# A planned transformer-and-experts kernel: two steps of the attention on GpSimd for four images, and a planner with stretched lengths and a table of bonuses

## What is computed

```python
x = x + linear_attention(ln_c(x))     # q softmax over 32 dims, k softmax over tokens, rmsnorm before and after
t = tokens(x)
t = t + moe(ln_t(t))                  # gate over 8 experts, the best two, 128 -> 256 -> gelu -> 128
out = images(t)
```

## Time and profile before

| | us |
|---|---|
| median of 3 runs | 775.15 (773.04 to 775.7) |
| profiled execution | 775.42 |
| its span | 773.7 |
| DVE busy in the span | 590.4 (76%) |
| PE busy | 654.0 (85%) |
| ACT busy | 536.7 (69%) |
| POOL busy | 481.6 (62%), of it 479.1 in 480 indirect DMAs |

### The profile page before, as it was taken

How to read it: one execution, slowest core, us unless ns; L and a number is a source line. 1 busy time by engine, 2 the same in 40 slices (tenths; PEclk the granted TensorE clock), 3 DMA queues, 4 the chain that set the end, 5 groups by cost and what they waited for, 6 DMA issues and landing times. The chain is left out here.

```text
span 773.7 us, 15758 instructions
## 1 busy us (share of the span) xinstructions
PE 654.0 (85%) x4074; PEld 545.7 (71%) x4074; DVE 590.4 (76%) x2178; ACT 536.7 (69%) x1388; POOL 481.6 (62%) x504
## 2 busy tenths in 40 slices
PE   4856489988989589999768899989689998699997
PEld 3534277866868367888566797876578887598896
DVE  5898989998999979997989899879885335642343
ACT  2633359667987549798737798868777775667775
POOL 1006553557646676776476777776777775677773
PEclk9978699998999889999978999999889999899999
DMA  6521466676756568697267788885499999537923
GB/s 170 154 90 62 148 204 199 204 235 175 224 155 198 171 208 238 198 316 216 100 202 214 223 284 244 272 269 166 124 276 323 319 325 322 185 102 216 315 81 109
DMA packets 110208, 159.28 MB, mean 206 GB/s; under 512 B 19216, under 2 KB 74536, under 8 KB 110120
## 3 DMA queue, kind: packets, MB, share of 16 engines
q1 hardware_dynamic: 93704, 126.58, 53.0%
q0 software_dynamic: 15360, 31.49, 13.5%
q10 hardware_dynamic: 1056, 0.22, 0.2%
HBM read 103.81 MB, written 57.02 MB: 208 GB/s over the span
## 5 line engine op out<-in xcount | busy, mean ns | idle before, releaser
L782 POOL DMA_INDIRECT rows_in<-xf_tok,row_of x240 | 243.4, 1014 | 199.0 <-DVE row_of L1343 108.3
L797 POOL DMA_INDIRECT y_rows<-rows_out,row_back x240 | 235.7, 982 | 81.1 <-issue 77.9
L1582 PE MATMUL y_ps<-wb,hid 128*128 128x128 f32 x1552 | 203.9, 278 | 13.7 <-ACT hid L899 12.5
L1582 PEld LDWEIGHTS y_ps<-wb,hid 128*128 128x128 f32 x1552 | 189.7, 192 | 27.9 <-ACT hid L899 22.7
L899 ACT ACTIVATE hid<-h_ps,wb 128x256 f32<-128x256 f32 x388 | 161.6, 474 | 52.8 <-PE h_ps L1572 32.1
L1572 PE MATMUL h_ps<-xt,wb 128*128 128x256 f32 x648 | 173.9, 396 | 6.4 <-DMA wb<-experts 4.5
L1572 PEld LDWEIGHTS h_ps<-xt,wb 128*128 128x128 f32 x648 | 116.6, 198 | 24.2 <-issue 6.0
L1410 DVE TENSOR_TENSOR yb<-y_ps,wb 128x256 f32<-128x256 f32 x162 | 68.1, 421 | 72.5 <-PE y_ps L1582 68.8
L1492 PE MATMUL ab<-wqkv_t,x_sb 128*128 128x392 f32 x256 | 105.6, 547 | 6.2 <-ACT qkv L837 5.7
L885 ACT ACTIVATE y_rows<-y_rows,share 128x128 f32<-128x128 f32 x240 | 83.2, 408 | 28.7 <-DMA y_rows<-rows_out,row_back 28.4
L837 ACT ACTIVATE qkv<-ab,root 128x392 f32<-128x392 f32 x128 | 71.2, 592 | 24.8 <-PE ab L1492 16.6
(11 more groups left out here) (195 smaller groups left out, 980.8 us busy)
## 6 DMA issues: line engine op xcount, KB each, us to landing
wb<-experts SPq DMA_DIRECT2D x162, 321.0 KB
xb<-rows_in SPq DMA_DIRECT2D x162, 128.0 KB
rows_out<-yb SPq DMA_DIRECT2D x162, 128.0 KB
rows_in<-zeros SPq DMA_DIRECT2D x69, 128.0 KB, 1.8
x_sb<-in_x_dram SPq DMA_DIRECT2D x16, 512.0 KB, 4.2
out_dram<-out_sb SPq DMA_DIRECT2D x32, 256.0 KB, 3.6
rows_in<-xf_tok,row_of POOLq DMA_INDIRECT x240
y_rows<-rows_out,row_back POOLq DMA_INDIRECT x240
```

What stands on the lines that cost most here:

```text
L782: pool.indirect_dma_start(out=rows_in[p % IN_BUFS], out_offset=bass.IndirectOffsetOnAxis(ap=row_of[:, n % X1_RING, k, t:t + 1], axis=0), i ...
L797: pool.indirect_dma_start(out=y_rows[:, r, k, :], out_offset=None, in_=rows_out[p % OUT_BUFS][0:BLOCKS[p] * ROWS, :], in_offset=bass.Indir ...
L1582: last = pe.matmul(y_ps[:, b % Y_BUFS, i * P:(i + 1) * P], hid[:, b % 2, k, i * P:(i + 1) * P], wb[:, r, HIDDEN + k * CH:HIDDEN + (k + 1) ...
```

## The change

1. For images 0 to 3 (`HELPED = 4`) `q_shift` and `q_norm` are issued on GpSimd instead of DVE: eight instructions in all. The planner takes them as 2.4 long there.
2. Every length is multiplied by a factor of its engine before planning (`PACE`).
3. `favour` adds a bonus per part of the program (`FAVOURED`, by image, group or dense expert) and one per kind of step (`FAVOURED_KIND`). The numbers go from -727 to 392.
4. A few steps get one more predecessor in the planner (`chain(...)`), the same step of the image before.

No other instruction is added or taken away. What each step computes and its buffers are unchanged.

```diff
+HELPED = 4
+PACE = {"PE": 1.08, "ACT": 1.1, "DVE": 1.1, "POOL": 1.035, "SP": 1.0}
+FAVOURED = {
+    "middle": (6.0, -68.8, 54.4, 21.4, 24.6, -37.8, 0.0, 0.9, -1.2, -12.9, 0.4, -89.8, -2.5, -1.3, 8.0, -19.7),
...
+FAVOURED_KIND = {
+    "C": 182.9, "D0": -2.6, "F1": 86.9, "F2": -26.0, "KB": -7.6, "KT": 3.4, "M": 4.9, "Q1": -38.6,
...
-        step("ACT", a("x_tok0"), 0.48, [a("X0")] + old("x1_1", TOK_RING), 0.2, table="any")
+        step("ACT", a("x_tok0"), 0.48, [a("X0")] + chain("x_tok1") + old("x1_1", TOK_RING), 0.2, table="any")
...
-        step("DVE", a("q_shift"), 1.14, [a("q_max")], 0.1)
+        step("POOL" if n < HELPED else "DVE", a("q_shift"), 2.4 if n < HELPED else 1.14, [a("q_max")], 0.12)
...
-        step("DVE", a("q_norm"), 1.14, [a("q_sum")], 0.1)
+        step("POOL" if n < HELPED else "DVE", a("q_norm"), 2.4 if n < HELPED else 1.14, [a("q_sum")], 0.12)
...
-        steps[name] = engine, length, more, [last_part.get(a, a) for a in after], bank, [last_part.get(a, a) for a in done or ()], table
+        steps[name] = engine, length * PACE[engine], more, [last_part.get(a, a) for a in after], bank, [last_part.get(a, a) for a in done or ()], table
...
 def favour(name):
 
-    if name[0] == "take":
-        return 500.0
-    return 0.0
+    part, i = part_of(name)
+    return (500.0 if name[0] == "take" else 0.0) + FAVOURED[part][i] + FAVOURED_KIND.get(name[0], 0.0)
...
+                if what == "q_shift":
+                    pool.wait_ge(s_q_max, n + 1)
+                    pool.tensor_tensor(queries(n), queries(n), stat_of_queries(0), ALU.subtract).then_inc(s_q_sub, 1)
+                if what == "q_norm":
+                    pool.wait_ge(s_q_sum, n * 2 + 2)
+                    pool.tensor_tensor(queries(n), queries(n), stat_of_queries(2), ALU.mult).then_inc(s_q_norm, 1)
```

More of the change, by code:

```diff
@@ L51 @@
 ROOT, SIZE, AHEAD = 10, 11, 0.15
+HELPED = 4
+PACE = {"PE": 1.08, "ACT": 1.1, "DVE": 1.1, "POOL": 1.035, "SP": 1.0}
+SETUP = ("load_w", "small", "experts", "ident", "center", "turn_w", "copy_w", "turn_s", "fold_gate", "fold_w", "turn_g", "fold_out",
+         "b1", "spare")
+EARLY = ("x_tok0", "x_tok1", "X0", "X1", "bn1_0", "bn1_1", "stats1", "load_x", "pair")
+LATE = ("logits0", "logits", "scores", "first", "exp", "choose", "count", "place", "xf0", "xf1", "stats2", "bn2_0", "bn2_1", "pair_r")
@@ new lines @@
+FAVOURED = {
+    "middle": (6.0, -68.8, 54.4, 21.4, 24.6, -37.8, 0.0, 0.9, -1.2, -12.9, 0.4, -89.8, -2.5, -1.3, 8.0, -19.7),
+    "back": (-15.2, -2.3, -62.5, -20.5, -51.5, 25.1, -86.2, -60.1, -8.0, 21.9, -17.7, -16.8, 4.1, 3.5, 93.8, 0.0),
+    "begin": (41.0,),
+    "block": (-68.3, -58.0, 1.7, -80.5, 0.0, -92.8),
+    "dense": (8.3, 2.8, -6.2, -29.1, 48.4, 1.9, 72.0, -69.3),
+    "early": (9.4, 46.1, -107.2, -17.3, -89.2, -109.2, 6.2, 95.6, 103.4, -13.4, 2.7, 3.6, 12.4, -38.3, 0.4, -2.2),
+    "fetch": (5.8, 0.4, 9.2, 4.4, 10.8, 12.1, -26.1, -7.8, -0.9, 0.0, 20.3, -8.1, -47.3, 19.7, 0.0, 0.0),
+    "join": (0.0, -103.5, -28.7, 67.0, 14.4, 0.0, -4.2, -6.9, -3.4, 112.4, 84.8, 11.4, 80.2, -1.4, 0.0, -0.1),
+    "late": (90.7, -157.3, -11.1, 28.2, 1.5, 0.5, -33.0, 69.9, -8.9, 10.4, 117.6, 90.7, -14.2, 25.9, -11.8, 0.0),
+    "send": (-15.3, -3.7, 0.0, -2.0, -14.1, -6.0, -120.5, 19.1, -28.3, -0.4, 0.4, -232.4, 0.0, 0.4, -28.3, 0.0),
+    "table": (-85.8, -5.5, 227.1, -56.9, 4.1, 0.0),
+}
@@ new lines @@
+FAVOURED_KIND = {
[3 rows of a table added]
+    "choose": -1.1, "count": -0.2, "ctx": 288.3, "ctx_t": 12.3, "cw_t0": -50.8, "cw_t1": -23.2, "down": -27.9, "exp": -66.9,
+    "exp_k": 47.6, "exp_q": 18.6, "experts": -3.9, "fetch": -218.1, "first": -727.0, "fold_gate": 57.5, "fold_out": 102.1, "fold_w": -16.1,
+    "gx": -20.2, "inverse": -48.8, "k_max": 14.5, "k_part": 0.2, "k_shift": 37.8, "load_w": 4.4, "load_x": -12.0, "logits": 2.3,
+    "logits0": -2.8, "mix": -2.0, "norm0": 391.8, "norm1": 29.8, "norm2": 387.3, "out": 10.4, "pair": 119.7, "place": -11.7,
+    "q_ch0": -19.2, "q_max": 1.0, "q_norm": 8.7, "q_sum": 1.7, "qkv0": 97.6, "qkv1": -49.9, "qkv2": 51.4, "qkv3": 129.0,
+    "qkv6": -50.3, "qkv7": 7.0, "root_s": -363.2, "scores": 71.3, "send": -10.7, "small": 13.4, "spare": 0.1, "square0": 2.5,
+    "square1": 12.4, "square2": 70.1, "stats1": 10.7, "stats2": 20.5, "store": -18.7, "store_out": -82.9, "table": -1.5, "take": 12.1,
+    "turn": -8.0, "turn_g": 71.9, "turn_s": -88.3, "turn_w": 9.7, "up": -120.1, "weigh": -0.1, "wload": -6.2, "x1_1": -181.1,
+    "x_ch0": -0.3, "x_ch1": -4.4, "x_tok0": -55.7, "x_tok1": 3.3, "xf0": 48.9, "xf1": -26.9, "xt": 129.9, "zero": 9.7,
+}
@@ L159, in attention @@
         step("PE", a("M"), 0.24, [a("ctx_t"), ("fold_out", 0)], 0.25, "M", [a("mix")])
-        step("DVE", a("mix"), 0.22, [a("M")] + old("F2", 2), 0.1)
+        step("DVE", a("mix"), 0.22, [a("M")] + chain("mix") + old("F2", 2), 0.1)
         for h, size in enumerate((0.71, 0.71, 0.48)):
@@ L169, in attention @@
         for h in range(2):
-            step("DVE", a(f"x1_{h}"), 0.6, [a(f"norm{h + 1}")] + ([a("x1_0")] if h else []), 0.1)
+            step("DVE", a(f"x1_{h}"), 0.6, [a(f"norm{h + 1}")] + ([a("x1_0")] if h else chain("x1_1")), 0.1)
             parts("DVE", a(f"bn2_{h}"), (0.39, 0.39), [a(f"x1_{h}")] + ([a("bn2_0")] if h else chain("stats2")), 0.1)
@@ L369, in bank_key, with part_of @@
     return (name[1], f"Y{name[2]}") if name[0] == "Y" else (name[1], name[0])
+def part_of(name):
+    kind, n = name[0], name[1]
+    if kind in ("send", "fetch", "table"):
+        return kind, n
+    if kind in ("weigh", "add"):
+        return "back", n
+    if kind in ("Y", "out", "store_out"):
+        return "join", n
+    if kind == "zero":
+        return "table", n
+    if kind in ("load", "turn", "xt", "store"):
+        return "block", group_of_block(n)
+    if kind in ("up", "gelu", "down", "take", "wload"):
+        dense, q, e, _ = JOBS[WLOADS[n] if kind == "wload" else n]
+        return ("dense", DENSE.index(q) * EXPERTS + e) if dense else ("block", group_of_block(q))
+    if kind in SETUP:
+        return "begin", 0
+    if kind in EARLY:
+        return "early", max(0, min(BATCH - 1, n))
+    return ("late" if kind in LATE else "middle"), n
 def favour(name):
-    if name[0] == "take":
-        return 500.0
-    return 0.0
+    part, i = part_of(name)
+    return (500.0 if name[0] == "take" else 0.0) + FAVOURED[part][i] + FAVOURED_KIND.get(name[0], 0.0)
 START, BANK_OF, ENGINE_OF, END = lay_out()
@@ L801, in fetch, with queries, stat_of_queries @@
                     ).then_inc(s_fetched[r], 16)
+            def queries(n):
+                return qkv[:, n % QKV_RING, :, Q_COL:K_COL].rearrange("p t (h d) -> p t h d", d=HEAD_DIM)
+            def stat_of_queries(k):
+                return q_stat[:, k, :].rearrange("p (t h) -> p t h", h=HEADS).unsqueeze(3).broadcast_to((P, TILES, HEADS, HEAD_DIM))
             pool.wait_ge(s_const, POOL_CONSTS)
-            for what, n, t in in_order("POOL"):
+            for what, n, *t in in_order("POOL"):
                 if what == "send":
-                    send(n, t)
+                    send(n, t[0])
                 if what == "fetch":
-                    fetch(n, t)
+                    fetch(n, t[0])
+                if what == "q_shift":
[4 more added lines that the diff above has]
+                    pool.tensor_tensor(queries(n), queries(n), stat_of_queries(2), ALU.mult).then_inc(s_q_norm, 1)
         @block.scalar
```

2 lines of the change are left out of this document (1 added, 1 removed), and 2 rows, old and new, of the table FAVOURED_KIND.

## The result

In its first measurement the changed kernel was slower: 783.31 us, the median of 4 runs (781.27 to 787.04), beside 774.1 for the kernel before; ratio 1.0126, 95% interval 1.0073 to 1.0178. The two intervals do not overlap, so a ratio of one set of runs is good to about half a per cent only, whatever its own interval says. Neither is the 0.988 that was forecast.

What follows compares the result with a forecast made beforehand. Bound: DVE up to 528 us, PE to 655, then POOL. Image 13's sends at 518.3, plus 132.3, 102.75 and 11.3, gain 9.0 us: 775.4 - 9.0 = 766.4, forecast 766; range 747 to 779 us.

Steps and rivals of the forecast that it cites:

- image 13's sends begin: POOL's sends of the fifth group's last image: predicted to start at 518.3 us instead of 528.4.
- from there to the first of the last 80 fetches: POOL's 102 DMAs from image 13's first send on: predicted 132.3 us, leaving POOL no wait ahead of the fetches.
- the last 80 fetches: POOL's third phase, fetches of the fifth group issued without a pause: 102.75 us, 1.28 each, same in both lists.
- tail: Weighing, adding, transposing, copying and storing behind the last fetch: 11.3 us, unchanged.
- I take 1 us of time for 1 us of work: DVE's phase: 10.1 us less work ahead of image 13's sends was taken to bring them equally earlier.
- company: Rival: each of the eight steps on POOL holds DVE 2.26 us, 18 us come back, 784.5 us; chance 0.05.
- POOL cannot set the pace here: Up to 528 us: POOL idles 59.5, 5.8 and 18.0 us waiting for DVE's row_of, so DVE is the bound.
- PE's way is 131.2 us as before: From image 13's sends through the fifth group's blocks to the first of the 80 fetches, PE needs an unchanged 131.2 us.
- The rest of the reordering: Stretched lengths and bonuses across the lists: idle time made or removed taken as zero, bounds 19 us either way.
- The early lag is never made up: Rival: the first group's blocks begin 14 us later and PE cannot catch up, 780.4 us; chance 0.11.
- The costs of POOL's own part: The eight moved steps, taken as 2.26 us each on POOL, fit inside its early waits and cost nothing there.
- signs of being wrong: Wrong if the 80 fetches begin later than 657, DVE's instructions beside POOL's are longer, or PE ends last.

Runs made afterwards that it cites:

- e13: The change itself, unaltered, measured again in 12 runs: 779.67 us, 1.0025 of the kernel before.
- e9: The change with SP's stores of blocks 145 and 146 moved ahead of two weight loads and one output store: 776.81 us, 1.0002 of before.
- e18: e9 with SP's zeroing of the last group's tails moved back, behind the store of block 134: 778.65 us, 1.0049 of before.
- e3: The change's lists held fast, but the eight q_shift and q_norm steps issued on DVE instead of POOL: 777.06 us, 1.0004 of before.
- e5: e3, with POOL waiting at its eight places for the end of DVE's steps and doing nothing there: 778.14 us, 0.9995 of before.
- e7: e3 with SP's stores of blocks 145 and 146 moved ahead of two weight loads and one output store: 772.23 us, 0.9915 of before.
- e12: e7 with SP's load of the first image moved ahead of that of the weights: 772.15 us, 0.9957 of before.
- e17: e7 with SP's zeroing of the last group's tails moved back, behind the store of block 134: 775.74 us, 1.0005 of before.
- e8: The change's lists with the four q_shift on POOL and the four q_norm on DVE: 779.72 us, 1.0041 of before.
- e14: e7 with q_shift 0 and 3 and q_norm 0 and 1 back on POOL, where DVE reduces or waits: 772.76 us, 0.9941 of before.
- e11: e7 with three unread products on PE ahead of each of seven kinds of early step, until the first block: 771.24 us, 0.9942 of before.
- e15: e7 with both the first image loaded ahead of the weights and the added unread products on PE: 772.39 us, 0.9974 of before.
- e6: e5 plus an unread two-input 128x1024 operation on POOL behind each of the eight waits: 789.9 us, 1.0158 of before.
- e10: As e6, but POOL does a memset of 128x2048 at each of its eight places: 777.13 us, 1.0047 of before.

## Why the prediction was wrong

The sum's own places, predicted and measured (the profiled execution of the change, and of e13):

| step | predicted | after | e13 |
|---|---|---|---|
| image 13's sends begin | 518.3 | 528.3 | 526.2 |
| from there to the first of the last 80 fetches | 132.3 | 144.1 | 143.2 |
| the last 80 fetches | 102.75 | 102.0 | 102.0 |
| tail | 11.3 | 9.1 | 9.1 |

**The step "I take 1 us of time for 1 us of work" failed.** It put the sends of image 13 at 518.3 us; they began at 528.3. DVE had 9.8 us less to do, and nothing of it arrived. Image 3's sends begin on the mean at 177.6 us in four executions with the eight steps on POOL (after 183.0, e13 179.5, e9 173.9, e18 174.2) and at 177.5 in five with them on DVE (e3, e5, e7, e12, e17: 176.7 to 178.9). The same two groups begin image 13's sends at 522.7 and 519.0 on the mean. The runs say that the steps on POOL cost more than they save: e18 over e17 0.4%, e9 over e7 0.9%, e13 over e3 0.2%. Only the second pair's intervals stand apart, but all three go one way: about 4 us of loss in place of 9.8 of gain.

Two things are seen to take the gain. First, company: 7.9 us of stretched instructions. I had this as a rival, but gave it 0.05 and said "No row shows such a thing": there was no elementwise work on POOL to show it, and I took silence for evidence. That its 784.5 us lies beside the profiled 785.2 is chance: 7.9 of its 18.1 us were paid, and the rest of the distance has other sources. Second, in the new order DVE was not bound by its work early on. The window of 24.6 to 140 us, where the eight steps lie, before and in e3:

```profile
24.60:140.00 115.40, 83.17 (x439) 61.18 (x437) 104.96 (x399) 61.53 (x162) 41.59 (x42) 0.87 0.46 144
```

```profile
24.60:140.00 115.40, 78.35 (x364) 54.20 (x363) 98.40 (x377) 53.38 (x136) 32.91 (x33) 0.81 0.35 111
```

and DVE's waits there in after:

```profile
DVE q_stat L1056 <- ACT qkv L906: 11.0, 4, 5.5
DVE k_recip L1086 <- PE ab L1573: 3.5, 2, 1.8
DVE qkv L1071 <- PE ab L1568: 2.8, 2, 1.9
DVE power L1265 <- ACT square L930: 2.1, 1, 2.1
```

DVE idles 10.4 us of this window before, 17.0 in e3 and 23.1 in after (busy 92.29 there). The idle time varies with the execution (e13 20.3, e9 13.8 and e18 13.5 us), but the new order has more of it in each. A narrower window of the kernel before would not have warned me: DVE is busy 91% of it there, for 89% of the long one. What failed was to take DVE's bound from the old lists for the new ones.

The same holds for POOL. "POOL cannot set the pace here" was read from the kernel before, where POOL still waited at 376.20 us; in after its last wait of over 1 us ahead of the 80 fetches ends at 283.32:

```profile
376.20 1.00 POOL L782 DMA_INDIRECT rows_in<-xf_tok,row_of  x1 [11.07 <-issue]
```

```profile
281.24 0.96 POOL L839 DMA_INDIRECT rows_in<-xf_tok,row_of  x1 [10.38 <-issue]
283.32 0.97 POOL L839 DMA_INDIRECT rows_in<-xf_tok,row_of  x1 [1.11 <-issue]
```

From there 185 DMAs stand ahead of image 13's sends, 1.32 us each, back to back. So in the new order DVE can bring these sends forward only by what it gains ahead of 283 us, and the eight steps gained nothing there.

Where the further loss of some 4 us comes from stays open. It is not in the early stretch: the two groups above are level at image 3, and from there to image 13's sends the one takes 345.1 us and the other 341.5 (e8, with four steps on POOL, 348.4; e14, also four, 345.6), though the last of the eight steps is over by 135 us. One rival is untested: TensorE's granted clock over a whole run was 0.936 on the mean in e9, e13 and e18 and 0.941 in e3, e7 and e17. Over all runs of the kernel before 0.01 of clock goes with 4.0 us of time by a straight line, so by estimate about half of the loss goes with the lower clock; whether as its cause or its effect no run here shows.

**The step "PE's way is 131.2 us as before" failed as badly.** From image 13's sends on the new order needs 12 to 13 us more, on e3's lists as on the change's. POOL's 102 DMAs fit: they end at 662.1, 133.8 us behind the first of them (132.3 predicted), ahead of the wait of 10.21 us. The loss is spread over the whole of PE's way:

| us | before | after | e3 | e7 |
|---|---|---|---|---|
| image 13's sends to the first product of block 108 | 33.5 | 37.6 | 37.0 | 37.4 |
| to the end of DVE's eviction of block 146 | 93.2 | 98.7 | 99.9 | 101.0 |
| to the first of the 80 fetches | 4.5 | 7.7 | 7.1 | 3.8 |

The last row is the stores' place: e7 has all of its 3 us back, and loses 1 of them again in the blocks, so that some 2 us are left. For the other two rows there is a trace, and no proof: DVE's waits between 560 us and 660 us (670 in after), before and then after:

```profile
DVE yb L1410 <- PE y_ps L1582: 35.6, 29, 3.4
```

```profile
DVE yb L1479 <- PE y_ps L1651: 19.8, 19, 2.6
DVE yb L1479 <- DMA rows_out<-yb: 8.3, 4, 4.1
DVE x_tok L1504 <- ACT y_rows L954: 7.1, 4, 5.0
```

Waits for the landing of a store are new. Moving the zeroing did not remove them, so what makes the stores late, and the first product of the group 4 us later, stays open.

**The rest of the reordering, put at zero,** was right in its sum (e3: 1.0004) and wrong in its parts: 16 us behind at image 3, 9 ahead at image 13, and all of that lost by the last fetches. What it gained in between is POOL's waiting: from 284 us to the wait ahead of the 80 fetches POOL had waited 20.5 us before and 2.1 in e3, counting waits of over 0.4 us. That e3 meets my 518.3 with 519.6 is chance; the order did it, not DVE's relief.

**The rival "The early lag is never made up"** is refuted by e3 as it was put: the new order makes up its lag on the old one. But among executions of the new lists an early lag stays, as the fifteen profiled executions above show. The costs of POOL's own part held: 1.91 us a step (2.26 taken), hidden in its waits (e5: 0.9995). The last fetches held to 0.8 us; the tail came out 2.2 us shorter. Two of the three signs of being wrong came: the 80 fetches began later than 657, and DVE's instructions beside POOL's were longer.

## The version that came out best

The change's lists with the steps back on DVE and the two stores first: e7, e11, e12, e14, e15 and e17 hold it with small additions (e14 has four of the steps on POOL) and stand at 0.9915, 0.9942, 0.9957, 0.9941, 0.9974 and 1.0005, 0.9956 on the mean: 0.4% faster than before, little more than can be told from nothing, and 0.7 to 1.7% faster than the change.

## What to carry to other kernels

Time taken off the busiest engine counts only where that engine has no waits of its own, and a change of order moves these waits: an engine that is the bound in the old order need not be in the new one (DVE idled 10.4 us from 24.6 to 140 us before and 17.0 in e3). Where the order changes too, measure the new order first with the old placement (e3), and look there for each engine's last wait. Elementwise work on GpSimd was not free of charge on VectorE (7.9 us of stretched instructions for eight steps here); ask of each moved step which VectorE instruction will stand beside it. And test a planner's change with the lists held fast, since the three new plans here stood 2 to 4% above the kernel before, far more than the edit was worth.

## What the runs showed of the hardware

In after and e6 a two-input GpSimd operation of 128x1024 (1.91 and 2.36 us) held VectorE's two-input instructions with both inputs in SBUF, and its TENSOR_SCALAR, until it ended: instructions of 0.15 to 0.3 us became up to 2.7 (`tab_b` 2.68 for 0.27 in after, a TENSOR_SCALAR 2.31 for 0.16 in e6), and a `q_shift` of 1.22 us took 2.01 (37.34 in e6). In e10 a GpSimd memset of 128x2048 (1.80 us) held TENSOR_SCALAR (`plan`, 1.79 us for 0.17 at 83.95) and CAST (`row_of`, 0.93 for 0.18 at 131.87), and what stood behind them, but not a TENSOR_TENSOR (`gate_x`, 0.21 us at 111.80; `placed`, 0.29 at 131.14). Neither held TENSOR_REDUCE (`k_part`, 1.94 us at 40.06 in e6, 1.90 at 40.08 in e10), BATCH_NORM_STATS2 (two of them 0.48 us at 36.88 in e6 and at 37.70 in e10) or a `k_shift` whose second input is in PSUM (1.22 us at 47.10 in e6 and at 46.67 in e10).

Two kinds of cases do not fit. Instructions that began together with GpSimd's operation were not held in e6: a TENSOR_SCALAR (`plan`, 128x15) that began 0.02 us behind that of 86.00 us kept its 0.17 us, though it was held beside the memset in e10, and `placed`, with two inputs in SBUF, kept its 0.29 us at 72.98. And twice in after the hold began 0.6 us ahead of GpSimd's operation, while it still issued a send (`tab_b` at 83.57, the send from 83.18 to 84.15; `gate` at 132.09, 2.64 us for 0.23, the operation at 132.71). I have no run that explains either.

Executions of one kernel differed by up to 2.0% (e10: 770.4 to 785.8 us), mostly in step with TensorE's granted clock: of e9's twelve runs one took 771.2 us at a mean clock of 0.947, one 785.1 at 0.927. In the profiled executions the clock differs most in the first 140 us: from 24.6 to 140 us it was 0.72 in the change and 0.84 in e9, whose lists are the same up to there, with image 3's sends at 183.0 and 173.9. Which of the two, clock or lag, drives the other isn't shown.
